# An attention and gated feed-forward layer on one core: rows of shifts sent by ScalarE's queue, every row masked on VectorE, loads and last steps in another order

## The chip, the cores and the metric

The kernel runs on one core of a Trainium2 chip. The metric is the device time of one execution in microseconds (us), as the median of several runs; lower is better. A core has TensorE (PE, matrix products), VectorE (DVE), ScalarE (ACT), GpSimd (POOL) and SyncE (SP), which run their own instruction streams and meet at semaphores, and 16 DMA engines. Products land in eight PSUM banks of 128 x 512 words.

## The reference

The input x is [4, 512, 1024]: four batches of 512 rows. One layer is computed:

```python
x = x + layernorm(attention(layernorm(x)))
x = x + layernorm(ffn(layernorm(x)))

# attention: 32 query heads and 8 key/value heads of 32, rotary q and k, causal softmax, output product
qkv = x @ w_qkv.T + b_qkv
attn = softmax(where(causal, q @ k.T / sqrt(32), -1e20)); out = (attn @ v) @ w_o.T + b_o

# ffn: base product, plus the two best of 8 experts of rank 16, weighted by a softmax of the gate
result = x @ base_w.T + base_b + 2.0 * sum_e w_full[e] * (x @ lora_A[e].T) @ lora_B[e].T
```

## The kernel before

The 2048 rows are 16 tiles of 128 (`NT`). Each f32 product is made of three products of halves: a high part (`_h`, rounded to fp32r) and the rest (`_l`). So every operand is split by a ScalarE copy (high) and a subtraction on VectorE or GpSimd (low).

There are three stages. **Projection**, to about 300 us: for each batch five pairs of q/k columns and four v tiles; rotated q and k and v go to scratch in HBM. **Attention**, to about 620 us: 32 groups (4 batches x 8 key heads), one a step; a group's q and k come back from HBM into one of four slots (`load_group`). **Output and feed-forward**, to the end: tile by tile the output product, a layer norm, the gated feed-forward (`ffn`, in three column blocks `FFN_COLS`), its low-rank part (`lora`), a layer norm and the store.

A step of attention for group n, in the order that `ORDER` writes out for TensorE:
- R0 to R10 (`row_scores`, L1345): scores of group n+2 with queries on partitions, only to find each row's maximum (`maxima` on VectorE). Later groups are masked in that operation by adding the table `row_mask` (L1015). For groups 0 and 1, whose rows are computed amid the projection of the last batch ("priming"), TensorE adds the mask with one more product of the identity and `causal_r` (L1351), and VectorE takes a plain maximum (L1020).
- T (`shift_transpose`): the maxima of group n+1 are turned into rows, split by ScalarE (`shift_to_hi`, L810) and VectorE (`shift_lo`, L1027), and written by two DMAs (`load_shift`, L494, 8 KB each, SyncE's queue) as two more rows of q in that group's slot. So the scores come out with the maximum subtracted.
- S0 to S9 (`scores`, L1371): scores of group n with keys on partitions; three banks take turns, so each S waits for the exponential (`exps`, L837, ScalarE) of the S three before it.
- V0 to V3 (`weigh`, L1387) and D (`denominators`, L1407 to L1413) for group n-1: the weighted values, and the sums of exponentials, which GpSimd has masked (L699) and partly added (`add_keys`, L711).

R units and T go round four banks, so an R waits for the maximum four units before. In steps 1 to 24 ScalarE also casts a piece of w_o (`piece_hi`, L826) and GpSimd makes its low part. SyncE's queue holds all other DMAs: per step the store of the attention values and sums, the next group (960 KB), and w_o, the bias rows and feed-forward weights in given steps. The last two steps (30 and 31) put chunks of the first output tile between the scores (`ORDER_OUT`, O0 to O7), for which `split_att` (ScalarE L844, VectorE L1097) must have split the attention values.

## Time and profile before

| | us |
|---|---|
| median of 3 runs | 1037.3 (1036.18 to 1037.53) |
| the profiled execution | 1043.99 |
| its span | 1042.3 |
| TensorE's mean granted clock | 0.988 |

Times below are from the span's start of the profiled execution. An instruction's duration includes latency that overlaps the next one, so the pace is read from start to start. The granted clock is a share of 2.4 GHz: 0.50 is the lower level, 1.2 GHz. The profile has three stretches in which it is near that: from 306 us, from 402 us and from 620 us, each of a few us.

### The profile page before, as it was taken

Reading aid. Unit: us, or ns where it says so; the run is one execution under the profiler, and the core shown is the slowest. Engines: PE = TensorE matmul, PEld = TensorE weight load, DVE = VectorE, ACT = ScalarE, POOL = GpSimd, SP = SyncE. Lnnn points to the kernel's source line nnn. Section 1 sums busy time; section 2 is a strip of 40 time slices with the busy share of each in tenths; the row PEclk is TensorE's granted clock in tenths of the full one; section 3 lists DMA queues with packets and bytes.
Section 4 is the critical chain, followed back from the end, with each engine's and each line's share of the span. In section 5 each row is a group of like instructions: output and inputs, shape, how many; then the busy total and the mean of one; then the engine's idle time right before and its main releaser. Section 6 shows DMA issues by size and latency. Waiting matters only on the chain.

```text
span 1042.3 us, 17345 instructions
## 1 busy us (share of the span) xinstructions
PE 1008.5 (97%) x6414; PEld 823.2 (79%) x6414; DVE 638.7 (61%) x1882; ACT 400.9 (38%) x682; POOL 452.3 (43%) x492
## 2 busy tenths in 40 slices
PE   6999999999989998999999989999999999999995
PEld 6888898898876665666666559999999999999995
DVE  6753533334447886788888747666666666666654
ACT  6331221200126775777777754222222222222221
POOL 1453443523337986899998851111111111111110
PEclk9999999999989998999999999999999999999998
DMA  9342431246236766656555455222222222222101
GB/s 356 138 143 102 146 132 66 91 146 178 81 135 175 205 186 161 162 138 172 141 138 138 121 176 170 79 81 83 82 87 80 84 80 74 84 82 79 53 21 40
DMA packets 78787, 127.29 MB, mean 122 GB/s; under 512 B 7792, under 2 KB 47088, under 8 KB 75632
## 3 DMA queue, kind: packets, MB, share of 16 engines
q1 hardware_dynamic: 78704, 126.19, 40.4%
q8 instruction: 51, 0.84, 0.3%
q14 instruction: 32, 0.26, 0.1%
HBM read 85.27 MB, written 40.37 MB: 121 GB/s over the span
## 4 chain that ended last, share of the span: by engine, by line
PE 92%; DVE 3%; DMA 2%; POOL 1%; ACT 1%; issue 0%; SPq 0%; POOLq 0%; DVEq 0%; ACTq 0%
PE bank L1272 21%; PE bank L1274 21%; PE bank L1273 20%; PE bank L1345 8%; PE bank L1371 7%; PE bank L1387 7%; DMA q_t<-shift_l 2%; PE bank L1281 2%; PE bank L1407 2%; PE bank L1529 1%; PE bank L1413 1%; PE bank L1410 1%; DVE bank L1015 1%; DVE ln_st L953 1%; POOL ln_rs L655 0%
## 5 line engine op out<-in xcount | busy, mean ns | idle before, releaser
L1015 DVE CUSTOM_DVE_ANT_0 bank<-bank,row_mask 128x128 f32<-128x128 f32 (+1 forms) x480 | 219.5, 523 | 61.1 <-PE bank L1345 57.1
L655 POOL TENSOR_TENSOR ln_rs<-ln_ve,minus_half 128x1 f32<-128x1 f32 x64 | 61.5, 961 | 394.6 <-DVE ln_mm L958 394.6
L837 ACT ACTIVATE prob<-bank 128x512 f32<-128x512 f32 x320 | 173.8, 598 | 44.8 <-PE bank L1371 44.7
L1272 PE MATMUL bank<-wf_h,xt_h 128*128 128x384 f32 (+1 forms) x384 | 129.7, 338 | 1.8 <-DVE z L1178 1.8
L1274 PE MATMUL bank<-wf_l,xt_h 128*128 128x384 f32 (+1 forms) x384 | 130.2, 339 | 0.0
L1273 PE MATMUL bank<-wf_h,xt_l 128*128 128x384 f32 (+1 forms) x384 | 129.6, 338 | 0.0
L1345 PE MATMUL bank<-k_t,q_t 96*128 96x384 f32 (+3 forms) x512 | 126.1, 343 | 3.0 <-DVE row_top L1015 3.0
L1272 PE MATMUL bank<-xt_h,wq_h 128*128 128x512 f32 x304 | 120.5, 397 | 0.0
L1274 PE MATMUL bank<-xt_l,wq_h 128*128 128x512 f32 x304 | 118.7, 390 | 0.0
L1273 PE MATMUL bank<-xt_h,wq_l 128*128 128x512 f32 x304 | 118.5, 390 | 0.0
L1371 PE MATMUL bank<-q_t,k_t 98*128 98x512 f32 x320 | 113.3, 418 | 5.2 <-DMA q_t<-shift_l 4.6
L1345 PEld LDWEIGHTS bank<-k_t,q_t 96*128 96x128 f32 x512 | 85.1, 195 | 24.4 <-DVE row_top L1015 15.0
L699 POOL TENSOR_SCALAR_AFFINE_SELECT prob<-prob 128x512 f32<-128x512 f32 x128 | 81.1, 645 | 50.1 <-ACT prob L837 49.9
L1272 PE MATMUL bank<-wo_h,at_h 128*128 128x512 f32 x256 | 101.3, 396 | 0.0
L1274 PE MATMUL bank<-wo_l,at_h 128*128 128x512 f32 x256 | 100.1, 391 | 0.0
L1273 PE MATMUL bank<-wo_h,at_l 128*128 128x512 f32 x256 | 100.0, 390 | 0.0
L780 ACT CAST turn_h<-turn 128x512 fp32r<-128x512 f32 x40 | 24.9, 622 | 163.5 <-POOL turn L669 151.9
L711 POOL TENSOR_TENSOR key_sum<-prob 128x512 f32<-128x512 f32 x64 | 82.0, 1288 | 8.5 <-ACT prob L837 8.5
L914 ACT ACTIVATE z<-z,ln_nm,ln_rs 128x1024 f32<-128x1024 f32 (+1 forms) x17 | 20.2, 1196 | 161.4 <-POOL ln_nm L657 161.4
L1371 PEld LDWEIGHTS bank<-q_t,k_t 98*128 98x128 f32 x320 | 59.2, 194 | 28.3 <-ACT prob L837 12.9
L711 POOL TENSOR_TENSOR key_sum<-key_sum,prob 128x512 f32<-128x512 f32 x63 | 81.5, 1313 | 0.0
L669 POOL TENSOR_TENSOR turn<-turn 128x512 f32<-128x512 f32 x20 | 25.8, 1292 | 126.5 <-DVE turn L991 126.5
(118 smaller groups left out, 1944.8 us busy)
## 6 DMA issues: line engine op xcount, KB each, us to landing
q_t<-q_scratch SPq DMA_DIRECT2D x32, 512.0 KB, 5.3
q_scratch<-turn_h SPq DMA_DIRECT2D x16, 512.0 KB, 2.7
q_scratch<-turn SPq DMA_DIRECT2D x16, 512.0 KB, 2.9
q_t<-q_scratch SPq DMA_DIRECT2D x32, 256.0 KB, 5.5
att_scratch<-att SPq DMA_DIRECT2D x32, 256.0 KB, 2.4
at_raw<-att_scratch SPq DMA_DIRECT2D x16, 512.0 KB, 3.9
x<-x SPq DMA_DIRECT2D x16, 512.0 KB, 4.2
out<-z SPq DMA_DIRECT2D x15, 512.0 KB, 2.9
```

Of the source, the lines that this page charges most:

```text
L655: nc.gpsimd.tensor_tensor(ln_rs[j][:], ln_ve[j][:], minus_half[:], ALU.pow).then_inc(count, 1)
L669: nc.gpsimd.tensor_tensor(r[:, 0, 0, :], r[:, 0, 0, :], r[:, 0, 1, :], ALU.subtract).then_inc(rope_sum, 1)
L699: nc.gpsimd.affine_select(out=block_of, in_=block_of, compare_op=ALU.is_ge, fill=0.0, base=0, pattern=[[0, REP], [1, P]], channel_multipli ...
L711: nc.gpsimd.tensor_tensor(total, first, prob[n % 2][:, b, :, :], ALU.add).then_inc(prob_summed, 1)
L837: nc.scalar.activation(prob[n % 2][:, i, :, :].rearrange("p h q -> p (h q)"), bank[3 + (NS * n + i) % 3][:], ACT.Exp, scale=INV_SQRT_HD).t ...
L1015: last = nc.vector.tensor_tensor_reduce(out=row, in0=row, in1=row_mask[:, SEQ - w:SEQ], scale=1.0, scalar=LOWEST, op0=ALU.add, op1=ALU.max ...
L1272: mm(dst, a_h, w_h, start=start, stop=False, skip_group_check=True)
L1273: mm(dst, a_l, w_h, start=False, stop=False, skip_group_check=True)
L1274: return mm(dst, a_h, w_l, start=False, stop=stop, skip_group_check=True)
L1345: last = mm(dst[:, w * at:w * at + w], q_t[s][0:KROWS, h, P * qb:P * qb + P], k_t[s][0:KROWS, 0:w], start=(at == 0), stop=masked_later(n, ...
L1371: mm(bank[3 + (NS * n + i) % 3][:].rearrange("p (h q) -> p h q", q=P), k_t[s][0:KROWS + 2, P * kc:P * kc + P], q_t[s][0:KROWS + 2, :, P * ...
L1387: last = mm(bank[6][HD * h:HD * h + HD, P * kc:SEQ].rearrange("p (b q) -> p b q", q=P), v_sb[b % 2][:, kc, HD * g:HD * g + HD], prob[n % 2 ...
```

## The change

- Causal mask: the products with `causal_r` go, all rows are masked in VectorE's maximum; `row_mask` is loaded before the first groups, in a place of its own.
- `load_shift` leaves SyncE's stream. ScalarE waits for `shift_sb` and issues the two DMAs on its own queue, behind the fourth exponential of a step.
- The score banks are turned by one and step 0 waits for the last v tiles later (at its third score).
- Loads of step 8 and 10 are put in steps 9, 11 and 13; the reciprocals of a batch's sums and their store move two and three steps.
- Step 30: S7 ahead of O0; ScalarE's `split_att(0)` behind the copy of values, the shifts and exponential 5; VectorE's behind `shift_lo`.
- After step 31: one sum less on GpSimd (D takes two more blocks directly, `FIRST[2]` and the next), VectorE waits for both of GpSimd's layer norm operations, ScalarE's and VectorE's feed-forward splits stand later.
- Feed-forward: `lora_ps` counts column blocks, `ffn` waits per block; the last tile runs blocks 0 and 1, their low-rank part, then block 2, and VectorE takes half of the statistics before block 2.

The diff, cut to its core:

```diff
-ORDER_OUT = [("S0 S1 S2 V0 V1 V2 V3 T S3 S4 S5 D S6 O0 S7 O1 S8 O2 S9 O3 "
-              "O4 O5 O6 O7").split(),
+ORDER_OUT = [("S0 S1 S2 V0 V1 V2 V3 T S3 S4 S5 D S6 S7 O0 S8 O1 S9 O2 "
+              "O3 O4 O5 O6 O7").split(),
...
             if s == SLOTS - 1:
+                row_mask = m("row_mask", [P, SEQ])
                 m = Map(e_at + SPILL, e_size - SPILL)
...
-        def masked_later(n, i):
-
-            return n >= 2
+        def score_bank(n, i):
+
+            return bank[3 + (NS * n + i + 1) % 3]
...
-            def load_shift(n):
-                s = n % SLOTS
-                sp.wait_ge(shift_sb, n + 1)
-                for i, part in enumerate((shift_h, shift_l)):
-                    dst = q_t[s][KROWS + i:KROWS + i + 1, :, :].bitcast(F32)
-                    sp.dma_start(dst, part[n % 2][:].bitcast(F32)).then_inc(shift_loaded[s], 16)
...
                     if b == BATCH - 1 and p == 0:
+                        sp.wait_ge(proj_ps, 2 * USES * (BATCH - 1))
+                        sp.dma_start(row_mask[:], row_mask_h).then_inc(mask_loaded, 16)
                         for n in range(SLOTS):
                             load_group(n)
...
-                    if b == BATCH - 1 and p == 3:
-                        load_shift(0)
...
-            sp.wait_ge(proj_ps, PROJECTED)
-            sp.dma_start(row_mask[:], row_mask_h).then_inc(mask_loaded, 16)
             load_v(0)
...
                 elif t == 1:
+                    sp.wait_ge(row_max, NR * NG)
                     sp.wait_ge(score_ps, NS * (NG - 1))
...
-                if n + 1 < NG:
-                    load_shift(n + 1)
...
-                if n >= KV and n % KV == 2:
+                if n >= KV and n % KV == 5:
                     store_inverses(n // KV - 1)
...
-                if n == WO_LOADS:
+                if n == WO_LOADS + 1:
                     sp.dma_start(bo_row[:], b_o[0].partition_broadcast(P)).then_inc(late_loaded, 16)
+                if n == WO_LOADS + 3:
                     sp.dma_start(bf_row[:], b_ffn[0].partition_broadcast(P)).then_inc(late_loaded, 16)
-                if n == WO_LOADS + 2:
+                if n == WO_LOADS + 5:
...
+            load_res(0)
             sp.wait_ge(score_ps, NS * NG)
             load_ffn(3)
             sp.dma_start(before[:], before_h[0].partition_broadcast(P)).then_inc(late_loaded, 16)
-            load_res(0)
...
-                add_keys(n, 2, total[:, 1, :, :], None, SCORES.index((2, 3)))
                 if n < NG - 1:
+                    add_keys(n, 2, total[:, 1, :, :], None, SCORES.index((2, 3)))
                     add_keys(n, 3, total[:, 0, :, :], None, FIRST[2])
...
+            def load_shift(n):
+
+                s = n % SLOTS
+                act.wait_ge(shift_sb, n + 1)
+                for i, part in enumerate((shift_h, shift_l)):
+                    dst = q_t[s][KROWS + i:KROWS + i + 1, :, :].bitcast(F32)
+                    act.dma_start(dst, part[n % 2][:].bitcast(F32)).then_inc(shift_loaded[s], 16)
...
+            load_shift(0)
...
                 exps(n, 2)
-                if n == NG - 2:
-                    split_att(0)
                 if 0 < n < NG - 1:
                     copy_values(n - 1)
                 if n + 1 < NG:
                     shift_to_hi(n + 1)
                 exps(n, 3)
+                if n + 1 < NG:
+                    load_shift(n + 1)
                 exps(n, 4)
                 if 1 <= n <= NPIECE:
                     piece_hi(n - 1)
                 exps(n, 5)
+                if n == NG - 2:
+                    split_att(0)
...
             split_ffn(3)
+            normalise_x1(0)
             copy_sums(NG - 1)
+            transposed2(0)
             split_ffn(4)
-            normalise_x1(0)
             split_ffn(5)
-            transposed2(0)
...
-            nc.vector.tensor_copy(ident_r[:], ident[:]).then_inc(const_ready, 1)
-            nc.vector.tensor_copy(causal_r[:], causal[:]).then_inc(const_ready, 1)
...
                 s = 9 * t
-                dve.wait_ge(lora_ps, t + 1)
                 wait(dve, out_stored, 16 * t)
                 for b, (at, w) in enumerate(FFN_COLS):
                     lo = max(at, AGW)
+                    if t == NT - 1 and b == 2:
+                        dve.wait_ge(z_step, s + 2)
+                        nc.vector.bn_stats(ln_st[1][:, 0, :], z[:, 0:HALF]).then_inc(z_step, 1)
+                    dve.wait_ge(lora_ps, 3 * t + b + 1)
...
+                if t == NT - 1:
+                    dve.wait_ge(z_step, s + 4)
+                    nc.vector.bn_stats(ln_st[1][:, 1, :], z[:, HALF:D]).then_inc(z_step, 1)
+                    moments(1, z_step, s + 3)
...
                 maxima_of(0, 1, 2)
+                if n + 1 < NG:
+                    shift_lo(n + 1)
                 if n == NG - 2:
                     split_att(0)
-                if n + 1 < NG:
-                    shift_lo(n + 1)
                 maxima_of(3, 4, 5)
-                if n >= KV and n % KV == 2:
+                if n >= KV and n % KV == 4:
                     invert_sums(n // KV - 1)
...
-            dve.wait_ge(y_scale, 1)
+            dve.wait_ge(y_scale, 2)
             split_att(1)
             split_ffn(2)
             residual1(0)
-            dve.wait_ge(y_scale, 3)
+            dve.wait_ge(y_scale, 4)
             split_ffn(3)
-            split_ffn(4)
             project_bias(1, 0)
             lo2(0)
+            split_ffn(4)
...
-                              start=(at == 0), stop=masked_later(n, i), skip_group_check=True)
-                if masked_later(n, i):
-                    last.then_inc(row_ps, 1)
-                    return
-                diagonal = dst[:, 0:len(heads) * w].rearrange("p (h k) -> p h k", k=w)[:, :, P * qb:w]
-                mm(diagonal, ident_r[:], causal_r[:].unsqueeze(1).broadcast_to([P, len(heads), P]), start=False,
-                   stop=True, skip_group_check=True).then_inc(row_ps, 1)
+                              start=(at == 0), stop=True, skip_group_check=True)
+                last.then_inc(row_ps, 1)
...
                     if n == 0:
                         pe.wait_ge(k_ones, SLOTS)
-                        pe.wait_ge(evac, EVACS * BATCH)
+                if n == 0 and i < 3:
+                    pe.wait_ge(evac, EVACS * BATCH if i == 2 else evacs(USES * (BATCH - 1) + PAIRS))
...
-                pe.wait_ge(prob_summed, SUMS * n + (SUMS if n < NG - 1 else 3))
+                pe.wait_ge(prob_summed, SUMS * n + (SUMS if n < NG - 1 else 2))
...
-            def ffn(t):
-                wait(pe, z_step, 9 * (t - 1) + 3)
-                for b, (at, w) in enumerate(FFN_COLS):
+            def ffn(t, blocks=range(3)):
+                for b in blocks:
+                    at, w = FFN_COLS[b]
+                    wait(pe, z_step, 9 * (t - 1) + b + 1)
...
-                ffn(t)
+                if t < NT - 1:
+                    ffn(t)
+            ffn(NT - 1, (0, 1))
             transpose_low(NT - 1)
-            lora(NT - 1)
+            lora(NT - 1, (0, 1))
+            ffn(NT - 1, (2,))
+            lora(NT - 1, (2,))
```

On ScalarE, step 1 of attention, before (numbers behind names tell buffers apart: prob_126 and prob_123 are the same buffer of the two programs):

```order
L837 ACTIVATE prob_126<-bank 128x512 x3
L854 COPY att_123<-bank 128x512
L810 ACTIVATE shift_h_76<-bank 16x128
L837 ACTIVATE prob_126<-bank 128x512 x2
L826 CAST wo_h<-wo_raw 128x384
L837 ACTIVATE prob_126<-bank 128x512
L859 COPY den_sb<-bank 128x512
L837 ACTIVATE prob_126<-bank 128x512 x4
```

and now:

```order
L831 ACTIVATE prob_123<-bank 128x512 x3
L848 COPY att_120<-bank 128x512
L795 ACTIVATE shift_h_74<-bank 16x128
L831 ACTIVATE prob_123<-bank 128x512
L804 DMA q_t_113<-shift_h_74 1x16x128
L804 DMA q_t_113<-shift_l_76 1x16x128
L831 ACTIVATE prob_123<-bank 128x512
L820 CAST wo_h<-wo_raw 128x384
L831 ACTIVATE prob_123<-bank 128x512
L853 COPY den_sb<-bank 128x512
L831 ACTIVATE prob_123<-bank 128x512 x4
```

The two DMAs, and the wait for VectorE's low part in front of them, stand between the fourth and fifth exponential; they stood on SyncE's stream. On ScalarE, step 30, before:

```order
L837 ACTIVATE prob_120<-bank 128x512 x3
L844 CAST at_h<-at_raw 128x1024
L854 COPY att_124<-bank 128x512
L810 ACTIVATE shift_h_77<-bank 16x128
L837 ACTIVATE prob_120<-bank 128x512 x3
L859 COPY den_sb<-bank 128x512
L837 ACTIVATE prob_120<-bank 128x512 x4
```

and now:

```order
L831 ACTIVATE prob_118<-bank 128x512 x3
L848 COPY att_121<-bank 128x512
L795 ACTIVATE shift_h_75<-bank 16x128
L831 ACTIVATE prob_118<-bank 128x512
L804 DMA q_t_116<-shift_h_75 1x16x128
L804 DMA q_t_116<-shift_l_77 1x16x128
L831 ACTIVATE prob_118<-bank 128x512 x2
L838 CAST at_h<-at_raw 128x1024
L853 COPY den_sb<-bank 128x512
L831 ACTIVATE prob_118<-bank 128x512 x4
```

`at_h`, from which the output product starts, has moved behind the copy of values, the shifts, the DMAs and three exponentials. On TensorE, the last tile's end, before:

```order
L1274 MATMUL bank<-wf_l_149,xt_h 128x384
L1548 MATMUL bank<-ident,low 128x128
L1272 MATMUL bank<-wo_h,low_h 128x256
L1273 MATMUL bank<-wo_h,low_l 128x256
L1274 MATMUL bank<-wo_l,low_h 128x256
L1272 MATMUL bank<-wo_h,low_h 128x384
L1273 MATMUL bank<-wo_h,low_l 128x384
L1274 MATMUL bank<-wo_l,low_h 128x384
L1272 MATMUL bank<-wo_h,low_h 128x384
L1273 MATMUL bank<-wo_h,low_l 128x384
L1274 MATMUL bank<-wo_l,low_h 128x384
```

and now:

```order
L1273 MATMUL bank<-wf_l_146,xt_h 128x384
L1545 MATMUL bank<-ident,low 128x128
L1271 MATMUL bank<-wo_h,low_h 128x256
L1272 MATMUL bank<-wo_h,low_l 128x256
L1273 MATMUL bank<-wo_l,low_h 128x256
L1271 MATMUL bank<-wo_h,low_h 128x384
L1272 MATMUL bank<-wo_h,low_l 128x384
L1273 MATMUL bank<-wo_l,low_h 128x384
L1271 MATMUL bank<-wf_h_137,xt_h 128x384
L1272 MATMUL bank<-wf_h_137,xt_l 128x384
L1273 MATMUL bank<-wf_l_145,xt_h 128x384
```

The transpose of `low` and six of the nine low-rank products now stand ahead of column block 2, whose first three products are the last rows shown; 21 more and block 2's three low-rank products follow.

## Rows read from the trace of the kernel before

**Rows 1.** Section 1 of the page: busy us (share of the span) and instructions of each engine.

```profile
PE 1008.5 (97%) x6414; PEld 823.2 (79%) x6414; DVE 638.7 (61%) x1882; ACT 400.9 (38%) x682; POOL 452.3 (43%) x492
```

**Rows 2.** Waits of TensorE over the span: line waited for, us in total, times, longest.

```profile
PE bank L1371 <- DMA q_t<-shift_l: 4.6, 4, 3.7
```

**Rows 3.** Stretch after the start of attention: us, then each engine's busy us, granted clock, DMA.

```profile
306.00:317.00 11.00, 10.62 (x36) 7.32 (x40) 8.65 (x38) 5.54 (x10) 7.36 (x8) 0.53 0.62 165
```

**Rows 4.** Chain that ended last, attention: start us, us, what ran.

```profile
324.14 0.69 PE bank L1345 x6
...
333.33 0.69 PE bank L1345 x6
...
351.70 0.69 PE bank L1345 x6
352.86 2.29 PE bank L1387 x32
...
425.00 0.69 PE bank L1345 x6
```

**Rows 5.** Timeline of one step, all engines: start, us, engine, line, operation, [idle before].

```profile
475.53 1.08 ACT L837 ACTIVATE prob<-bank 128x512 f32<-128x512 f32 x2 [0.32 <-PE bank L1371]
475.56 0.28 DVE L1027 SCALAR_TENSOR_TENSOR shift_l<-bank,shift_h 16x128 fp32r<-16x128 f32 x1
...
475.87 0.53 SPq L494 DMA_DIRECT2D q_t<-shift_h  x1
...
476.43 0.59 SPq L494 DMA_DIRECT2D q_t<-shift_l  x1
476.50 0.51 ACT L826 CAST wo_h<-wo_raw 128x384 fp32r<-128x384 f32 x1
...
477.70 0.59 ACT L859 COPY den_sb<-bank 128x512 f32<-128x512 f32 x1 [0.18 <-PE bank L1413]
...
478.18 1.16 ACT L837 ACTIVATE prob<-bank 128x512 f32<-128x512 f32 x2
...
478.78 0.62 PE L1371 MATMUL bank<-q_t,k_t 98*128 98x512 f32 x2
```

**Rows 6.** Timeline of TensorE in the projection of the last batch.

```profile
243.31 0.22 PE L1351 MATMUL bank<-causal_r,ident_r 128*128 128x128 f32 x1
243.37 0.45 PE L1272 MATMUL bank<-xt_h,wq_h 128*128 128x512 f32 x1
```

**Rows 7.** Timeline of VectorE at the start of attention.

```profile
304.90 0.30 DVE L1015 CUSTOM_DVE_ANT_0 bank<-bank,row_mask 128x128 f32<-128x128 f32 x1 [3.60 <-DMA row_mask<-row_mask]
...
307.39 0.28 DVE L1027 SCALAR_TENSOR_TENSOR shift_l<-bank,shift_h 16x128 fp32r<-16x128 f32 x1
```

**Rows 8.** Timelines at the end of attention: TensorE.

```profile
595.62 0.64 PE L1407 MATMUL bank<-prob,ones 128*32 128x256 f32 x8 [1.32 <-ACT att L854]
...
597.38 0.40 PE L1272 MATMUL bank<-wo_h,at_h 128*128 128x512 f32 x1
...
620.65 1.08 PE L1407 MATMUL bank<-prob,ones 128*32 128x256 f32 x8 [2.88 <-POOL key_sum L711]
...
623.80 0.60 PE L1272 MATMUL bank<-wo_h,at_h 128*128 128x512 f32 x1
```

**Rows 9.** Timeline at the end of attention: ScalarE.

```profile
593.94 1.05 ACT L844 CAST at_h<-at_raw 128x1024 fp32r<-128x1024 f32 x1 [1.91 <-DVE at_raw L1092]
```

**Rows 10.** Timeline at the end of attention: VectorE.

```profile
595.02 1.69 DVE L1097 TENSOR_TENSOR at_l<-at_raw,at_h 128x1024 fp32r<-128x1024 f32 x1 [1.11 <-ACT at_h L844]
```

**Rows 11.** Timeline of the last tile: TensorE.

```profile
1018.05 0.45 PE L1272 MATMUL bank<-wf_h,xt_h 128*128 128x392 f32 x1 [1.77 <-DVE z L1178]
```

**Rows 12.** Timeline of the last tile: VectorE.

```profile
1016.65 1.34 DVE L1178 TENSOR_TENSOR z<-bank,bf_row 128x256 f32<-128x256 f32 x3
...
1033.48 1.35 DVE L1178 TENSOR_TENSOR z<-bank,bf_row 128x256 f32<-128x256 f32 x3 [1.76 <-PE bank L1274]
1034.87 1.29 DVE L953 BATCH_NORM_STATS2 ln_st<-z 128x6 f32<-128x512 f32 x2
```

More of the change, by code:

```diff
@@ L122, in final_cols, with build @@
     return [slice(0, HALF), slice(HALF, D)] if t == NT - 1 else [slice(0, D)]
-def build(nc, x, w_qkv, b_qk, b_v, w_out, b_o, w_ffn, b_ffn, cos_t, sin_t, ident_h, causal_h, row_mask_h, before_h, out):
+def build(nc, x, w_qkv, b_qk, b_v, w_out, b_o, w_ffn, b_ffn, cos_t, sin_t, ident_h, row_mask_h, before_h, out):
     q_scratch = nc.dram_tensor("q_scratch", [BATCH, PAIRS - 1, 2, 2, P, SEQ], F32).ap()
@@ L953, in statistics, with moments @@
                     nc.vector.bn_stats(ln_st[j][:, h, :], src[:, HALF * h:HALF * h + HALF]).then_inc(count, 1)
+                moments(j, count, before_it)
+            def moments(j, count, before_it):
                 dve.wait_ge(count, before_it + 2)
@@ L1006, in maxima @@
                 w = P * (qb + 1)
+                if n == 0 and i == 0:
+                    dve.wait_ge(mask_loaded, 16)
                 dve.wait_ge(row_ps, NR * n + i + 1)
@@ L1009, in maxima @@
                     wait(dve, shift_ps, n - 1)
-                if masked_later(n, i):
-                    if n == 2:
-                        dve.wait_ge(mask_loaded, 16)
-                    for at, h in enumerate(heads):
-                        row = row_bank(n, i)[:, w * at:w * at + w]
-                        last = nc.vector.tensor_tensor_reduce(
-                            out=row, in0=row, in1=row_mask[:, SEQ - w:SEQ], scale=1.0, scalar=LOWEST,
-                            op0=ALU.add, op1=ALU.max, accum_out=row_top[n % 2][:, h, qb:qb + 1])
-                    last.then_inc(row_max, 1)
-                else:
-                    nc.vector.tensor_reduce(row_top[n % 2][:, heads[0]:heads[-1] + 1, qb],
-                                            row_bank(n, i)[:, 0:len(heads) * w].rearrange("p (h k) -> p h k", k=w), AX_X, ALU.max
-                                            ).then_inc(row_max, 1)
+                for at, h in enumerate(heads):
+                    row = row_bank(n, i)[:, w * at:w * at + w]
+                    last = nc.vector.tensor_tensor_reduce(
+                        out=row, in0=row, in1=row_mask[:, SEQ - w:SEQ], scale=1.0, scalar=LOWEST,
+                        op0=ALU.add, op1=ALU.max, accum_out=row_top[n % 2][:, h, qb:qb + 1])
+                last.then_inc(row_max, 1)
             def shift_lo(n):
@@ L1179, in ffn_sum @@
                                             ).then_inc(z_step, 1)
-                dve.wait_ge(z_step, s + 3)
-                statistics(z, 1, z_step, s + 3)
+                if t == NT - 1:
+                    dve.wait_ge(z_step, s + 4)
+                    nc.vector.bn_stats(ln_st[1][:, 1, :], z[:, HALF:D]).then_inc(z_step, 1)
+                    moments(1, z_step, s + 3)
+                else:
+                    dve.wait_ge(z_step, s + 3)
+                    statistics(z, 1, z_step, s + 3)
             def residual2(t):
@@ L1403, in denominators @@
                     pe.wait_ge(den_ready, n)
+                if n == 0:
+                    pe.wait_ge(const_ready, 1)
                 p, total = prob[n % 2], key_sum[n % 2]
@@ L1417, in denominators @@
                         dst = den_bank(n)[HD * h:HD * h + HD, :].rearrange("p (b q) -> p b q", q=P)
-                        last = mm(dst[:, 2:3, :], ones[:], p[:, FIRST[2]:FIRST[2] + 1, h, :], start=False, stop=True,
+                        last = mm(dst[:, 2:4, :], ones[:], p[:, FIRST[2]:FIRST[2] + 2, h, :], start=False, stop=True,
                                   skip_group_check=True)
@@ L1548, in transpose_low, with lora @@
                 nc.tensor.transpose(bank[7][:, 0:P], low[:].rearrange("p e r -> p (e r)"), ident[:]).then_inc(low_ps, 1)
-            def lora(t):
+            def lora(t, blocks=range(3)):
                 pe.wait_ge(low_ready, t + 1)
-                for b, (at, w) in enumerate(FFN_COLS):
+                for b in blocks:
+                    at, w = FFN_COLS[b]
                     lo = max(at, AGW)
@@ L1556, in lora @@
                                    False, True)
-                last.then_inc(lora_ps, 1)
+                    last.then_inc(lora_ps, 1)
             project_out(1, 0)
```

15 lines of the change are left out of this document (2 added, 13 removed).

## The prediction

> **What bounds the kernel now.** I read the page's busy shares first: TensorE is busy for 97% of the span [rows 1], so nothing counts unless it takes work from TensorE, fills one of its waits, or makes a new one. The list of TensorE's waits is next: behind the unavoidable start, the rows of shifts are its largest cause, 4.6 us in four waits [rows 2]. But a wait costs more than its length where the clock falls after it: from 306 to 317 us the granted clock is 0.53, near its lower level of 1.2 GHz, and what came before is TensorE's wait for the first maximum, which itself waited for the mask table [rows 3, 7]. So I measure stalls by the period of a step on the chain of waits. An undisturbed step takes 333.33 - 324.14 = 9.19 us. From 351.70 to 425.00 there are seven steps: 73.3 us where 64.3 are due, so the late shifts cost 9.0 us, clock included [rows 4]. In the timeline of a step I then look for what ScalarE has to spare, since the change gives it work.
>
> **The change part by part.** The sum is made against the profiled execution's 1043.99 us and taken off the median of 1037.3 us unchanged; the profile ran 6.7 us longer than the median, so some stalls in it may be the profile's own.
>
> Causal products (22 of them, 11 units for two groups). The next product starts 0.06 us after one of 128 columns, and that next one takes 0.45 us instead of the 0.40 of its kind, a weight load laid bare [rows 6]. 0.12 x 22 = 2.6 us, and 3.0 with the six that are 256 and 512 columns wide. Bounds: 0, if the place were a wait in disguise, and 22 x 0.22 = 4.8 by the whole duration. I take -3.0, as TensorE has no wait there. VectorE gets 32 masked maxima for 22 plain ones; the projection keeps TensorE the bound and VectorE waits for it there.
>
> Start of attention. The mask table is now loaded with the first groups, before the priming. VectorE's first maxima start where its wait of 3.60 us began, at 301.3, not at 304.90, and with them `shift_lo`: 307.39 - 3.6 = 303.8 [rows 7]. ScalarE then issues the DMAs for 1.15 us, to 305.0 (durations below), and has six exponentials of step 0 left at 0.51 each, start to start: 308.1. Step 1's weighted values wait for its S1 and S2, behind these: 308.8. Such a block starts 352.86 - 351.70 = 1.16 us after its step's first R, so step 2's first R stands at 308.8 - 1.16 + 9.19 = 316.8, and 317.4 with step 1's own share of the delay below, for 324.14 [rows 4]: -6.7. Bounds: 0 and -8.
>
> Shift stalls. Before, the two 8 KB DMAs stood in line behind a group's 960 KB and, around step 8, three more loads of 512 KB. Those are now in steps of their own, and the rows have their own queue. I take -8.0 of the 9.0; bounds 0 (all of it the profile's own, or carried over) and -9.0.
> The Trainium skill says on this, in "DMA: Bandwidth & Descriptors", section "Issuing engines are not separate DMA queues", that DMAs of all engines run on the same 16 DMA engines and interleave, and that using several saves the issuing time only. No row here shows two queues at once. By this rule the queue would cure nothing and the spreading of the loads alone most of it, so the sum would lose the small stalls (a rival below).
>
> ScalarE's new work. On SyncE the two issues last 0.53 and 0.59 us and follow each other: 475.87 to 477.02 [rows 5]. No row shows an issue on ScalarE; bounds are 0 and that 1.15. I take the latter. The DMAs wait for `shift_lo`, ended at 475.84. Exponential 4, the second of the pair at 475.53, began at 476.02 and would now at 477.05: 1.03 late. Behind it the cast, exponential 5, the copy of the sums and exponential 6 queue. ScalarE had 0.18 us idle before that copy, so 0.85 is left at exponential 6, which ended at 478.18 + 0.60 = 478.78. S9, the second of the pair at 478.78, starts at 479.01 and needs it, 0.23 later. So TensorE stops for 0.62 us in each such step. It is not carried on: behind the weighted values ScalarE sits idle, and starts the next step level. Of the steps with a cast, 2 to 24 count here: 23 x 0.62 = 14.3. The five without (25 to 29) have the cast's 0.51 to spare: 5 x 0.1 = 0.5. Together +14.8; bounds 0 and 28 x 1.03 = 28.8.
> "Perfetto Trace Analysis" of the Trainium skill, section on the HWDGE DMA instruction, has the profiled window of an issue end when the sequencer is free for the next instruction. The trace agrees on SyncE, where the next issue starts 0.03 us behind the first. By the rule ScalarE loses the whole 1.15 us, as in the sum; were it free of this, the sum would be that of the second rival.
>
> Step 30. D no longer waits for ScalarE's copy, which was held by `at_h` (1.32 us goes) [rows 8]. But `at_h` moves from 593.94 [rows 9] behind the shifts (594.2 to 594.5), their DMAs (595.65) and exponentials 4 and 5: 596.7. `at_l` starts at its end, took 1.69 us and, beside less of GpSimd's work, may take somewhat less [rows 10]: 599.2. O0 stood at 597.38 and, with S7 (0.23 us) now in front of it, would stand at 599.2: a net +1.6. TensorE waits there from 596.6, 2.6 us. A wait of that length has lowered the clock twice [rows 3, 8]; the last of these made D take 3.15 us (620.65 to 623.80) for some 1.6 at full clock, so +1.5. Bounds +0.5 and +4.
>
> After step 31. D waited 2.88 us for GpSimd's last sum and ran at the lower clock; it would start at 617.8 and end at 619.5, for 623.80 [rows 8]: -4.3. What is late next is `at_l` of tile 1, held by `ln_nm` now: 618.5, in time. Bounds -1 and -5.
>
> Last tile. `ffn` waits for one of three additions (0.45 of 1.34 us): -0.9 of the 1.77 [rows 11, 12]. At the end two of three additions and one of two statistics (0.9 + 0.65) are hidden by block 2's 24 products: -1.5 [rows 12]. Together -2.4, bounds -1 and -3.
>
> The rest (reciprocals, loads' places, constants) I cost at nothing: VectorE and SyncE are not the bound there. If that cover fails, it costs a fraction of a us four times.
>
> Sum: -3.0 - 6.7 - 8.0 + 14.8 + 3.1 - 4.3 - 2.4 = -6.5. 1043.99 becomes 1037.5, and 1037.3 becomes 1030.8 us.
>
> **The rivals.**
> The issue is cheap on ScalarE. For it: no row shows it there. Against: two issues on SyncE never overlap. The +14.8 goes, and the total is -21.3: 1016.0 us.
>
> ScalarE becomes the bound. Should the idle time before the copy and S9's 0.23 not absorb anything, or an issue take longer where SyncE issues too, the delay per step grows. The gains are 21.3 us over 28 steps: from 0.76 us a step on the kernel is slower. With the whole 1.03, it is 28.8 - 21.3 = +7.5: 1044.8 us. For it: ScalarE's instructions from exponential 4 to 6 stand without a gap but one. Against: the 0.18 and 0.23 us are measured.
>
> The rows land no sooner. Large loads on the same engines delay them as before; the stalls around step 8 may go by the spread loads, the others stay, and where they were the profile's own nothing goes: between -8.0 and 0. With 0 the total is +1.5: 1038.8 us. Against: the small stalls too stand where the queue is full.
>
> The start does not gain: step 0 has thin work on TensorE, the clock may fall there anyway. It took 11 us at 0.53; I price it at +2.5: 1033.3 us.
>
> **How the numbers follow.** Chances: forecast, with the thin start in it, 0.55; cheap issue 0.17; ScalarE the bound 0.16; rows no sooner 0.12. A measurement of this kernel can tell about 0.2%, 2 us. The forecast's own range is 1025 to 1037; 0.47 of its 0.55 lies more than 2 us under 1037.3, 0.06 within, 0.02 above. Cheap issue is all faster. The bound case is slower, 0.14, or the same, 0.02. Rows no sooner: 0.04 faster, 0.06 the same, 0.02 slower. Faster 0.68, same 0.14, slower 0.18. The range for 8 in 10 runs from 1017 to 1042: it leaves out the cheapest issue and the worst delay.
>
> **What would show it.** ScalarE's DMA issues would have durations near 0.5 us, exponential 4 would start about 1 us behind the issue, and TensorE would show 23 waits near 0.6 us for ScalarE's exponential, a period near 9.8 us up to step 24, and 9.2 to 9.3 from 25 on. No wait for the shift rows, and none for the mask. No L1351. A wait of about 2.6 us before the first product of the output with a low clock behind it; none before D of group 31. The last addition would follow the last product by 0.2 us and half of the statistics would be gone from the tail. I am wrong if the period stays 9.19 (cheap issue), or reaches 10.2.

## The result, and the profile after

The changed kernel takes **1047.93 us** in the median of 6 runs (1046.74 to 1050.94). The kernel before, run beside it, takes 1037.41 us (1035.17 to 1040.05). The ratio is 1.0104, with a 95% interval of 1.0084 to 1.0124: slower by 1%, where 1030.8 us and a gain were forecast, and above the range of 1017 to 1042. The profiled execution took 1048.65 us (span 1046.9), 4.7 more than the one before. That one ran 6.6 us above its own median, so the traces show less of the loss than the times do.

Section 1 of the page after, first line; then two lines of the list of TensorE's waits, in the columns of [rows 2]:

```profile
PE 1009.8 (96%) x6392; PEld 815.0 (78%) x6392; DVE 645.2 (62%) x1922; ACT 398.5 (38%) x682; POOL 446.6 (43%) x491
```

```profile
PE bank L1365 <- ACT prob L831: 11.2, 27, 0.5
...
PE bank L1365 <- DMA q_t<-shift_l: 1.7, 3, 1.1
```

TensorE has 22 products fewer than in [rows 1], and as much busy time. The wait for the shift rows of [rows 2] has shrunk from 4.6 to 1.7 us. A new wait stands on top: 27 times, 0.41 us on average, for ScalarE's exponential.

The chain of waits after, read as [rows 4]: step 2, and then three neighbouring steps with a cast.

```profile
317.10 0.68 PE bank L1343 x6
...
376.73 0.69 PE bank L1343 x6
...
386.61 0.68 PE bank L1343 x6
...
396.47 0.69 PE bank L1343 x6
```

Step 2 starts at 317.10, where 324.14 stood before. That this is next to the forecast's 317.4 is luck: the 317.4 held the gain of the start alone, and with the 3.0 us of the causal products it should have been 314.4. But above all a step now lasts 386.61 - 376.73 = 9.88 us instead of 9.19. The timeline of such a step shows why; the columns are those of [rows 5]:

```profile
483.99 0.60 ACT L831 ACTIVATE prob<-bank 128x512 f32<-128x512 f32 x1 [0.32 <-PE bank L1365]
484.02 0.28 DVE L1022 SCALAR_TENSOR_TENSOR shift_l<-bank,shift_h 16x128 fp32r<-16x128 f32 x1
...
484.33 0.51 ACTq L804 DMA_DIRECT2D q_t<-shift_h  x1
...
484.87 0.61 ACTq L804 DMA_DIRECT2D q_t<-shift_l  x1
...
485.52 0.60 ACT L831 ACTIVATE prob<-bank 128x512 f32<-128x512 f32 x1 [0.94 <-issue]
...
486.02 0.50 ACT L820 CAST wo_h<-wo_raw 128x384 fp32r<-128x384 f32 x1
...
486.42 0.60 ACT L831 ACTIVATE prob<-bank 128x512 f32<-128x512 f32 x1
...
486.91 0.58 ACT L853 COPY den_sb<-bank 128x512 f32<-128x512 f32 x1
...
487.38 2.08 ACT L831 ACTIVATE prob<-bank 128x512 f32<-128x512 f32 x4
...
487.23 0.40 PE L1365 MATMUL bank<-q_t,k_t 98*128 98x512 f32 x1
488.05 0.50 PE L1365 MATMUL bank<-q_t,k_t 98*128 98x512 f32 x1 [0.41 <-ACT prob L831]
```

This is the mechanism that was forecast. ScalarE issues for 0.51 and 0.61 us. Exponential 4 starts 0.04 us behind the second issue and 0.94 us later than it could have. The cast, exponential 5 and the copy pass the delay on, and the score product S9 waits for exponential 6, which began at 487.38. The wait of 0.41 us costs more than its length: S9 starts 0.82 us behind S8 (487.23) where it was 0.23 before (478.78 and 479.01), and lasts 0.50 us instead of 0.40. Together that is the 0.69 us.

At the start of attention the wait for the mask table goes, as was expected. First the window of [rows 3], then VectorE's maxima and `shift_lo`, as in [rows 7], then TensorE in front of step 1:

```profile
306.00:317.00 11.00, 9.87 (x85) 6.12 (x86) 7.56 (x34) 6.80 (x15) 7.77 (x9) 1.00 0.47 117
```

```profile
299.08 0.30 DVE L1014 CUSTOM_DVE_ANT_0 bank<-bank,row_mask 128x128 f32<-128x128 f32 x1 [0.21 <-PE bank L1343]
...
301.57 0.27 DVE L1022 SCALAR_TENSOR_TENSOR shift_l<-bank,shift_h 16x128 fp32r<-16x128 f32 x1
```

```profile
306.72 0.50 PE L1365 MATMUL bank<-q_t,k_t 98*128 98x512 f32 x1 [1.06 <-DMA q_t<-shift_l]
```

The wait for the table is gone, and the granted clock stays at its upper level, 1.00 where it was 0.53. What the prediction lacked is the last line: it let step 1 start as soon as ScalarE's exponentials were done and expected no wait for the shift rows, but the low row, issued at 302.42, landed 4.3 us later, and TensorE waited for it.

The end of attention after: TensorE, which answers to [rows 8]; ScalarE and VectorE, [rows 9, 10]; and one window with the granted clock.

```profile
601.55 0.64 PE L1403 MATMUL bank<-prob,ones 128*32 128x256 f32 x8 [1.11 <-POOL key_sum L696]
...
605.57 0.71 PE L1271 MATMUL bank<-wo_h,at_h 128*128 128x512 f32 x1 [1.85 <-DVE at_l L1088]
...
627.27 0.64 PE L1403 MATMUL bank<-prob,ones 128*32 128x256 f32 x8
...
629.13 0.50 PE L1271 MATMUL bank<-wo_h,at_h 128*128 128x512 f32 x1
```

```profile
602.87 1.05 ACT L838 CAST at_h<-at_raw 128x1024 fp32r<-128x1024 f32 x1
```

```profile
603.95 1.57 DVE L1088 TENSOR_TENSOR at_l<-at_raw,at_h 128x1024 fp32r<-128x1024 f32 x1 [3.28 <-ACT at_h L838]
```

```profile
603.00:610.00 7.00, 5.15 (x18) 3.78 (x15) 3.93 (x2) 3.58 (x6) 4.87 (x5) 0.76 0.26 78
```

O0 waits 1.85 us for `at_l`, and D had to wait 1.11 us for GpSimd before it; a lower clock follows, as forecast. D of group 31 waits for nothing and is done in 1.86 us, for 3.15 in [rows 8].

The last tile after, TensorE and VectorE, for [rows 11, 12]:

```profile
1023.89 0.45 PE L1271 MATMUL bank<-wf_h,xt_h 128*128 128x392 f32 x1 [0.86 <-DVE z L1172]
```

```profile
1034.30 1.02 DVE L1172 TENSOR_TENSOR z<-bank,bf_row 128x256 f32<-128x256 f32 x2 [0.78 <-PE bank L1273]
1035.35 0.69 DVE L1169 BATCH_NORM_STATS2 ln_st<-z 128x6 f32<-128x512 f32 x1
...
1039.48 0.56 DVE L1172 TENSOR_TENSOR z<-bank,bf_row 128x384 f32<-128x384 f32 x1 [3.44 <-PE bank L1273]
```

Two additions and one of the statistics now lie beside products, and `ffn` waits 0.86 instead of 1.77 us.

### The profile page after: what moved, and what is told of

It is laid out like the page before. It is cut to its first block, busy times and chain, and to the rows that moved or that the text cites. A ratio compares the mean times of both kernels' runs of the same rounds, so it can differ in the third digit from the quotient of the medians.

```text
span 1046.9 us, 17330 instructions
## 1 busy us (share of the span) xinstructions
PE 1009.8 (96%) x6392; PEld 815.0 (78%) x6392; DVE 645.2 (62%) x1922; ACT 398.5 (38%) x682; POOL 446.6 (43%) x491
## 4 chain that ended last, share of the span: by engine, by line
PE 83%; ACT 7%; DVE 3%; ACTq 2%; DMA 2%; issue 2%; POOL 1%; POOLq 0%; DVEq 0%
PE bank L1271 20%; PE bank L1273 20%; PE bank L1272 20%; PE bank L1381 7%; PE bank L1343 6%; PE bank L1365 5%; ACT prob L831 4%; ACTq L804 2%; DMA q_t<-shift_l 2%; PE bank L1280 1%; PE bank L1525 1%; ACT wo_h L820 1%; ACT den_sb L853 1%; POOL ln_rs L640 1%; DVE ln_st L949 1%
## 5 line engine op out<-in xcount | busy, mean ns | idle before, releaser
L1014 DVE CUSTOM_DVE_ANT_0 bank<-bank,row_mask 128x384 f32<-128x384 f32 (+3 forms) x512 | 236.0, 519 | 90.2 <-PE bank L1343 89.6
L831 ACT ACTIVATE prob<-bank 128x512 f32<-128x512 f32 x320 | 175.3, 610 | 68.7 <-PE bank L1365 38.6
L1365 PE MATMUL bank<-q_t,k_t 98*128 98x512 f32 x320 | 119.7, 423 | 13.1 <-ACT prob L831 11.2
L1343 PE MATMUL bank<-k_t,q_t 96*128 96x384 f32 (+3 forms) x512 | 123.5, 337 | 0.4 <-DVE row_top L1014 0.3
L1343 PEld LDWEIGHTS bank<-k_t,q_t 96*128 96x128 f32 x512 | 82.8, 190 | 21.6 <-DVE row_top L1014 7.9
L696 POOL TENSOR_TENSOR key_sum<-key_sum,prob 128x512 f32<-128x512 f32 x62 | 77.9, 1276 | 0.0
```

Source lines behind the costliest of these rows:

```text
L696: nc.gpsimd.tensor_tensor(total, first, prob[n % 2][:, b, :, :], ALU.add).then_inc(prob_summed, 1)
L831: nc.scalar.activation(prob[n % 2][:, i, :, :].rearrange("p h q -> p (h q)"), score_bank(n, i)[:], ACT.Exp, scale=INV_SQRT_HD).then_inc(pr ...
L1014: last = nc.vector.tensor_tensor_reduce(out=row, in0=row, in1=row_mask[:, SEQ - w:SEQ], scale=1.0, scalar=LOWEST, op0=ALU.add, op1=ALU.max ...
L1343: last = mm(dst[:, w * at:w * at + w], q_t[s][0:KROWS, h, P * qb:P * qb + P], k_t[s][0:KROWS, 0:w], start=(at == 0), stop=True, skip_group ...
L1365: mm(score_bank(n, i)[:].rearrange("p (h q) -> p h q", q=P), k_t[s][0:KROWS + 2, P * kc:P * kc + P], q_t[s][0:KROWS + 2, :, P * qb:P * qb ...
```

## The experiments

"Period" is the time from one step's first R to the next one's. "Excess" is the sum of the periods from step 2 on, less 9.19 us each (step 28 is the last with such a period): 8.9 us in the first profile of before and 21.6 us in that of after. What is left behind the last such mark is the "end part": 461.3 and 460.2 us.

**The shift rows back on SyncE (e1_syncq, and again e11_syncq_again).**

```diff
-                act.dma_start(dst, part[n % 2][:].bitcast(F32)).then_inc(shift_loaded[s], 16)
+                sp.dma_start(dst, part[n % 2][:].bitcast(F32)).then_inc(shift_loaded[s], 16)
```

with `load_shift(n + 1)` first in SyncE's step n, as before; all else stays as changed.

> The changed kernel with one thing undone: both rows of shifts are issued by SyncE again, at the start of a step; all else as changed. Theory A (each step's two issues keep ScalarE for 1.04 us, of which 0.69 us in steps with a cast and 0.27 us in those without reach TensorE, 17 us in all): the step is 9.19 us again, no wait of TensorE for ScalarE's exponentials, and the time falls by 17 us less the stalls that ScalarE's queue had removed (0 to 5): 1031 to 1036 us, under the kernel before. Rival B (the loss comes from the other edits: the turned banks, the spread loads, the masks, the last steps): the time stays within 3 us of 1048.

> The changed kernel with the rows of shifts issued by SyncE once more, beside the two others. 1022 to 1024 us, ratio 0.983 to 0.985. If step 30 in its new order costs something (the run with the old order had 0.9834), this ratio is over 0.9845; if it gains, under 0.983.

1022.91 us, ratio 0.9837 (0.9817 to 0.9857); measured again, 1022.36, ratio 0.9841 (0.9825 to 0.9857). So this one part of the change, the issuing engine, costs 25 us by the medians, 27 by the ratios, and without it the change is a gain of 1.6%. Both theories missed the size: theory A, which is right on the steps, had 1031 at the least. No kernel tried here is faster by more than can be told. The periods are 9.19 us again, the excess is 1.8 and 1.05 us, step 0 takes 7.16 us instead of 8.58, and the end part is 457.3 to 457.7. ScalarE's exponentials, from the fifth section of the pages, of after and of e1_syncq:

```profile
L831 ACT ACTIVATE prob<-bank 128x512 f32<-128x512 f32 x320 | 175.3, 610 | 68.7 <-PE bank L1365 38.6
```

```profile
L833 ACT ACTIVATE prob<-bank 128x512 f32<-128x512 f32 x320 | 173.3, 599 | 35.9 <-PE bank L1365 35.9
```

The idle time before them is 68.7 us with the issues on ScalarE and 35.9 without. Of the 68.7, the trace puts 30.0 down to "issue", the rest to TensorE.

**ScalarE's queue alone (e2_scalarq_alone):** the kernel before, with `load_shift` on ScalarE and nothing else.

> The kernel before with one thing done: the two rows of shifts are issued by ScalarE behind exponential 3; all else as before. Theory A: a step of 9.88 us with the cast and 9.47 without, +17 us, less the stalls of the kernel before that the queue removes (about 2 in an undisturbed run, up to 9): 1046 to 1053 us. Rival B: within 3 us of the kernel before, 1035 to 1040.

1062.49 us, ratio 1.0211 (1.0189 to 1.0232): 22 us more than before, above what either theory gave. The waits of TensorE, two lines:

```profile
PE bank L1371 <- ACT prob L835: 10.5, 25, 0.5
...
PE bank L1371 <- DMA q_t<-shift_l: 2.5, 1, 2.5
```

The periods are 9.88 with a cast, and two of 12.85 and 12.74 us stand at steps 9 and 10, with the granted clock low behind the wait. The excess is 24.7 us: 17.0 from the delay of each step, as in the changed kernel, and 7.7 from long steps. The end part is 464.9 us, some 4 us longer than in the two profiles of before: D of step 30 waits 2.1 us for GpSimd's sum, where it waited 1.3 for ScalarE's copy. Theory A had left out the end part and taken the queue to remove long steps. The rows had the queue to themselves and still landed late there. By the Trainium skill, "DMA: Bandwidth & Descriptors", section "Issuing engines are not separate DMA queues", DMAs issued by different engines run on the same 16 DMA engines and interleave. The trace agrees, with this wait of 2.5 us in spite of the rows' own queue.

**One row each (e3_half):** the changed kernel, `shift_h` issued by SyncE and `shift_l` by ScalarE.

```diff
-                for i, part in enumerate((shift_h, shift_l)):
+                for i, part in ((1, shift_l),):
```

> The changed kernel with one of the two rows (the high part) issued by SyncE and the other still by ScalarE. Theory A: ScalarE loses 0.5 to 0.6 us a step instead of 1.04, of which 0.18 idle before its copy and some 0.2 before the tenth score take most: at most 0.2 us reaches TensorE in a step with a cast, nothing without, so the step is 9.2 to 9.4 us and the time 1031 to 1038. A rival in which any issue on ScalarE stops it for a fixed time whatever it sends (a drain of its pipeline) expects the period of 9.88 to fall by half of 0.69 or less: 9.5 us or more, 1040 or more.

1024.28 us, ratio 0.9849 (0.9831 to 0.9867), period 9.25 with a cast and 9.19 without. The period is as theory A had it; its time, 1031 us or more, was too high, as in e1_syncq. One issue, of 0.52 us here, costs 0.06 us a step, two cost 0.69: ScalarE has spare time for nearly all of one, and only what exceeds it reaches TensorE. The rival of a fixed stop at any issue falls.

**The cast out of the way (e10_cast_late):** the changed kernel with both issues on ScalarE, and

```diff
                 exps(n, 4)
-                if 1 <= n <= NPIECE:
-                    piece_hi(n - 1)
...
                 for i in range(6, NS):
                     exps(n, i)
+                if 1 <= n <= NPIECE:
+                    piece_hi(n - 1)
```

> The changed kernel as it is, both rows of shifts issued by ScalarE, with one edit: the cast of a piece of w_out (0.50 us) stands behind the last exponential of the step, where ScalarE is idle, and no longer behind exponential 4. Theory A (the two issues delay exponential 6 by what they last less ScalarE's spare time before S9, so spare time given back is time gained): the periods of steps 2 to 24 fall from 9.88 to 9.47, as in the steps without a cast; 23 x 0.41 = 9.4 us, and some of the stalls with it: 1034 to 1039 us, ratio 0.995 to 1.000. Theory B (the issues cost by something else, as traffic or the clock): the periods stay at 9.8 to 9.9 and the time at 1045 to 1050.

1037.14 us in the median of 12 runs, ratio 0.999 (0.9978 to 1.0003): 10.8 us less than the changed kernel. The periods are 9.47 to 9.6 in most steps, and TensorE's list has a wait for an exponential twice instead of 27 times. The 0.28 us by which these steps still exceed 9.19 shows in the periods alone. Its waits, one line:

```profile
PE bank L1365 <- ACT prob L831: 0.9, 2, 0.5
```

Nothing about the DMAs differs, so theory B falls: it is ScalarE's time between exponentials 3 and 6 that counts.

**Spreading the loads alone (e5_spread_alone):** the kernel before, with `bo_row`, `bf_row`, `load_ffn(6)` and the inverses' store in later steps.

> The kernel before with one part of the change: bo_row, bf_row, load_ffn(6) and the inverses' store (with invert_sums) in later steps of their own; the rows of shifts stay on SyncE with everything else. The stalls of steps 8 to 12 took 8.9 us in the first profile of before and 3.2 us in its second. Theory A (they come from the rows standing in line behind these loads): the stalls go, the periods of all steps from 2 on are within 0.5 us of 9.19, and the time is 2 to 6 us below the kernel before, ratio 0.994 to 0.998. Theory B (rows are late for another reason, the 960 KB group and the chance order in the engines): stalls of 10 us and more remain near steps 9 to 11, ratio 0.999 to 1.001.

1033.74 us, ratio 0.9951 (0.9936 to 0.9966), 5 us faster. The wait for the shift rows in its trace:

```profile
PE bank L1372 <- DMA q_t<-shift_l: 0.2, 1, 0.2
```

The excess is 0.5 us, with the rows in SyncE's queue among all others. The stalls came from the loads that stood beside them, as theory A has it.

**The kernel before, profiled again (before_again).** One execution of 1035.58 us (span 1033.9) and the same wait:

```profile
PE bank L1371 <- DMA q_t<-shift_l: 2.2, 1, 2.2
```

The excess is 3.2 us, for 8.9 in the first profile. So 6 of the 9.0 us that the prediction wanted back were missing in this execution. It is quicker, though, than all nine executions of this kernel that were timed beside it (1037.95 to 1042.59), as the first profile is longer than any of them. The 5 us of e5_spread_alone, from medians, are the better measure of the stalls.

D of group 31 waits in it as in [rows 8], but does not run slowly, and the window around it has the upper clock:

```profile
612.90 0.64 PE L1407 MATMUL bank<-prob,ones 128*32 128x256 f32 x8 [2.88 <-POOL key_sum L711]
```

```profile
611.00:616.00 5.00, 3.10 (x38) 2.36 (x39) 1.96 (x3) 2.25 (x3) 1.80 (x1) 1.00 0.87 331
```

The next five undo one more part each (the last of them two) in the kernel with the rows on SyncE, which has 1022.36 us and ratio 0.9841 as its reference.

**Step 30 as before (e6_old_step30).**

```diff
-ORDER_OUT = [("S0 S1 S2 V0 V1 V2 V3 T S3 S4 S5 D S6 S7 O0 S8 O1 S9 O2 "
+ORDER_OUT = [("S0 S1 S2 V0 V1 V2 V3 T S3 S4 S5 D S6 O0 S7 O1 S8 O2 S9 O3 "
```

and both `split_att(0)` where they were.

> The changed kernel with the rows of shifts issued by SyncE, and step 30 as before: O0 in front of S7, ScalarE's split_att(0) behind exponential 2, VectorE's in front of shift_lo. Compared with the same kernel with the new step 30 (1022.9 us, ratio 0.9837). Theory A (the prediction's +3.1 for the new step 30, less about 0.6 since ScalarE no longer issues there): the old order is better, 1020 us, ratio 0.981, and the new one showed its clock drop in 603 to 610 as the cost. Theory B: what O0 waits for at_l is paid back by D no longer waiting for at_h, and the two orders are equal: 1022 to 1024, ratio 0.983 to 0.985. Theory C: the new order is better by 1 to 3 us: 1024 to 1026.

1022.01 us, ratio 0.9834 (0.9819 to 0.9848): no difference to be told. With SyncE issuing, O0 waits 1.3 us for `at_l` in the new order, and D waits 1.3 us for ScalarE's copy, held by `at_h`, in the old one. Theory B holds: the two waits are exchanged. D waits another 0.8 us for GpSimd in the new order; the end part is 456.4 us in the old order and 457.3 to 457.7 in the new, too little to show in the times.

**The work behind step 31 as before (e7_old_after31).**

```diff
-                if n < NG - 1:
-                    add_keys(n, 2, total[:, 1, :, :], None, SCORES.index((2, 3)))
+                add_keys(n, 2, total[:, 1, :, :], None, SCORES.index((2, 3)))
...
-                pe.wait_ge(prob_summed, SUMS * n + (SUMS if n < NG - 1 else 2))
+                pe.wait_ge(prob_summed, SUMS * n + (SUMS if n < NG - 1 else 3))
```

with the waits and splits of `w_ffn` behind it.

> The changed kernel with the rows of shifts issued by SyncE, and the work behind step 31 as before: GpSimd adds the third sum for group 31 and D waits for three sums, VectorE waits for y_scale 1 and 3, and the splits of w_ffn stand as before on ScalarE and VectorE. Theory A (the prediction's -4.3 for this part of the change): 1027 us, ratio 0.988, with a wait of 2 to 3 us before D and a lower clock behind it. Theory B (the profile of after gave back only 1.1 us in all from step 30 on, the waits move to ScalarE's normalised y): 1023 to 1025, ratio 0.984 to 0.986.

1025.07 us, ratio 0.9868 (0.9852 to 0.9884), between the two theories: the part is worth 2.7 us. D of group 31 in its timeline, and the window around it:

```profile
604.11 0.64 PE L1403 MATMUL bank<-prob,ones 128*32 128x256 f32 x8 [2.88 <-POOL key_sum L708]
...
605.76 0.50 PE L1271 MATMUL bank<-wo_h,at_h 128*128 128x512 f32 x1
```

```profile
603.41:608.41 5.00, 4.30 (x44) 3.33 (x45) 4.23 (x7) 1.56 (x2) 1.94 (x3) 1.00 0.84 300
```

The wait is exactly that of [rows 8], but the clock stays at 1.00 and D takes 1.65 us, not 3.15, just as in before_again, where the kernel is the same as in [rows 8]. The same window in the first trace of before:

```profile
620.00:625.00 5.00, 4.34 (x37) 2.61 (x38) 2.93 (x6) 1.71 (x3) 1.04 (x2) 0.66 0.69 270
```

The low clock behind such a wait is not a fixed part of its price.

**The last tile as before (e8_old_last_tile).**

```diff
-            ffn(NT - 1, (0, 1))
-            transpose_low(NT - 1)
-            lora(NT - 1, (0, 1))
-            ffn(NT - 1, (2,))
-            lora(NT - 1, (2,))
+            transpose_low(NT - 1)
+            lora(NT - 1)
```

with `ffn` in one piece, waiting for all three additions, and additions and statistics in one piece too.

> The changed kernel with the rows of shifts issued by SyncE, and the feed-forward's ends as before: ffn waits for all three additions of the tile before it, the last tile's three blocks go in one piece, its additions and statistics wait for the last of them. Theory A (the prediction's -2.4 for this part): 1025.3 us, ratio 0.986, the time behind the last product 1.5 us longer and the wait before ffn 0.9 longer. Theory B: only the end counts, 1.5 us, or the reordered last tile's products pay it back: 1023 to 1024.

1026.66 us, ratio 0.9882 (0.9869 to 0.9895): the part is worth 4.3 us, more than theory A's 2.4. The first product behind the wait, and the window behind it:

```profile
998.70 0.44 PE L1263 MATMUL bank<-wf_h,xt_h 128*128 128x392 f32 x1 [1.79 <-DVE z L1169]
```

```profile
999.50:1004.50 5.00, 5.00 (x21) 5.00 (x21) 2.11 (x5) 1.24 (x1) 0.74 (x2) 0.66 0.00 0
```

This time the clock did fall behind the wait, to 0.66 for 5 us, 1.7 us of work. In the trace of before the same wait left it at 1.00. The end part of this trace, 461.3 us, is 4.0 longer than in e1_syncq: 0.9 by the wait, 1.4 behind the last product, and these 1.7. So in this trace the clock accounts for what the part is worth beyond waits and tail. All four timed runs have the same mean granted clock, 0.996, as the profiled one, where the reference has 0.997 to 0.999, so it probably fell in all of them; but only one has a trace.

**The causal products back (e9_causal_products_back).**

```diff
+                diagonal = dst[:, 0:len(heads) * w].rearrange("p (h k) -> p h k", k=w)[:, :, P * qb:w]
+                mm(diagonal, ident_r[:], causal_r[:].unsqueeze(1).broadcast_to([P, len(heads), P]), start=False,
+                   stop=True, skip_group_check=True).then_inc(row_ps, 1)
```

for groups 0 and 1, with their plain maxima.

> The changed kernel with the rows of shifts issued by SyncE, and with the causal products of groups 0 and 1 and their plain maxima back; the mask table still comes early. Compared with the same kernel without them, run beside it. Theory A (the prediction's -3.0, 0.12 us and more for each of 22 products on TensorE while nothing waits): 3 us slower, 1026 us, ratio 0.9865, and the first R of step 0 stands at 301.5 to 302.5 instead of 298.4. Theory B (VectorE's 10 additional masked maxima had cost what the products save, the gain of the start is all from the early mask): less than 1 us apart. Step 0 takes 7.2 to 7.5 us in both by either theory, since the mask is no longer waited for.

1025.0 us, ratio 0.9868 (0.9853 to 0.9883): the products cost 2.6 us, as in theory A.

**The mask table late as well (e12_mask_late):** e9, with the load of `row_mask` behind the projection as before.

> As the kernel with the causal products of groups 0 and 1 back (1025.0 us, ratio 0.9868; rows of shifts on SyncE), and with the mask table's load where it stood before: behind the last product of the projection. Compared with that kernel, this is what the earlier mask alone is worth. Theory A (the prediction's -6.7 for the start): 1031 to 1032 us, ratio 0.993, with the wait of 3 us for the first maxima and the granted clock near 0.5 for some 10 us behind it. Theory B (the sum of the other parts as timed leaves only 2 to 3 us for it, since the first profile had the longest clock drop): 1027 to 1028.5, ratio 0.989 to 0.990; steps 0 and 1 together 18.9 to 20.5 us against 16.6.

1029.93 us, ratio 0.9914 (0.9898 to 0.993), 4.9 us above e9 and between the two theories. VectorE's first maximum there, and the window of [rows 3]:

```profile
305.07 0.30 DVE L1024 CUSTOM_DVE_ANT_0 bank<-bank,row_mask 128x128 f32<-128x128 f32 x1 [3.47 <-DMA row_mask<-row_mask]
```

```profile
306.00:317.00 11.00, 10.44 (x65) 7.29 (x65) 9.46 (x45) 6.43 (x13) 7.39 (x8) 0.84 0.65 187
```

The wait for the table is nearly that of [rows 7] (3.60), yet the clock fell to 0.84 here and to 0.53 there. The early mask takes the wait away in either case; how far the clock falls behind that wait varies.

## Why the prediction was wrong

**The step that failed: ScalarE's issue, +14.8 forecast, +25 measured** (25.0 and 25.6 by the two runs on SyncE). The mechanism was right and the size was not. The +14.8 stood for the steps from 2 on; there the trace of after and that of e1_syncq differ by 21.6 - 1.8 = 19.8 us.

Of these, 17.0 are the direct part, which was nearly right. The delayed steps lose 0.69 us (0.62 forecast) and the others 0.28 (0.1): 23 x 0.69 + 4 x 0.28 = 17.0. Both the late exponential 6 and the cast's share in it are shown, by e3_half and e10_cast_late.

The other 2.8 us are single long steps, which the prediction put at nothing with "It is not carried on". The traces show two causes. In steps 10, 13, 20 and 26 the second issue itself lasted 0.82, 1.33, 0.73 and 0.93 us instead of 0.61. In the last three of them the step is longer by just that excess: 0.72, 0.12 and 0.32 us (step 10 by 0.9 us, with waits of its own). Three steps of e2_scalarq_alone and one of e10_cast_late show the same, each to 0.01 us. On SyncE such an issue costs nothing: e1_syncq has one of 1.32 us in step 13, and that step lasts 9.19 us. And step 11 is 1.6 us longer, with a granted clock of 0.66 from 407 to 412 us, behind two waits of TensorE in step 10 (0.48 us for an exponential, 0.42 for the shift rows); e1_syncq has 1.00 all through attention.

The rest of the 25 us lies outside those steps: 1.4 us in step 0, 0.7 in step 1, and 3.0 in the end part. The latter is mostly the wait for `at_l` (1.9 for 1.3 us), D's for GpSimd (1.1 for 0.8) and the clock of 0.76 for 7 us (1.7 us), where e1_syncq has 1.00. The prediction had some of this, in its terms for the start and for step 30, so 14.8 should be set against 19.8, and not against the whole 25.

I had bounded the term at 28.8, so the size was in the bounds. But I gave the rival by which ScalarE becomes the bound 0.16 and a time of 1044.8; with the 25 us in place of 14.8, the sum of the prediction is +3.7, past break-even.

**Shift stalls, -8.0 forecast.** The spreading of the loads alone brought 5 us, and the queue none that its one trace shows: in e2_scalarq_alone the long steps stay. The prediction named both ways, the profile's own stalls and the rule on queues, and took the optimistic end. It sized the term on one long execution: the same kernel had 8.9 us of excess in one profile and 3.2 in the other.

**Causal products, -3.0:** 2.6 measured, right.

**Start of attention, -6.7:** the wait for the table went and the clock stayed at 1.00, as said, but the early mask is worth 4.9 us. Start and causal products together were to bring step 2 forward by 9.7 us; the traces have 324.14 - 317.10 = 7.0. Step 1 waited for the shift rows, a wait that the forecast's path had left out. The trace that it was sized on had the deepest fall of the clock of the five that have this wait: 0.53, where the others have 0.69 (e5_spread_alone) to 0.84 (e12_mask_late).

**Step 30, +3.1:** seen in the trace of after, O0's wait with a low clock behind it. With the rows on SyncE the wait is 1.3 us for 1.9, the clock stays at 1.00, and the new order costs nothing that can be told. The fall of the clock there came with the issues.

**After step 31, -4.3:** 2.7. The wait of 2.9 us went, as said. The 1.5 for the clock is not bound to it: e7_old_after31 and before_again have the same wait and D at full clock. And the next waits came up: 1.1 us for the normalised y and 0.5 for `low` in e1_syncq, which e7 has not or has at 0.2.

**Last tile, -2.4:** 4.3. The 0.9 of the wait and 1.4 of the tail are in the traces; the rest is likely the clock (1.7 in the trace of e8_old_last_tile), which was left out here and counted in for step 31.

The parts as timed are 5.1 + 2.6 + 4.9 + 2.7 + 4.3 = 19.6 us of gain, and all of them together gave 16 to 17; each has an interval of some 1.5 us. Against the 21.3 of the prediction that is 4 to 5 short, and the issue cost 10 more. Both errors are on the same side, the larger is the issue, and the 2 us still missing to the measured +10.5 lie within these intervals.

## What to carry to other kernels

Giving an engine DMAs to issue is giving it work: look for the engine's spare time between the issue and the next result that the bounding engine needs, and count what exceeds it in every step (one issue of 0.5 us cost 0.06 us a step here, two cost 0.69, and 25 us of 1048 in all). Size a gain on stalls and low clocks only from two profiles of the same kernel, since one execution here had 6 us of stalls that the next had not. And here the late rows were cured by taking away the loads that travelled beside them, not by another queue.

## What the runs showed of the hardware

An issue of one 8 KB row on ScalarE lasts 0.51 us for the first and 0.61 for the second (medians of 32), at most 1.33, and the next activation starts 0.04 us behind it. It holds up ScalarE's computing for its whole length, the long ones too: 1.33 us instead of 0.61 made the step 0.72 us longer.

The granted clock behind a wait of TensorE is not fixed by the wait. Behind the same wait of 2.9 us it stayed at 1.00 in e7_old_after31 and in before_again, and was 0.66 over 620 to 625 in the first trace of before, whose kernel is that of before_again. Behind 1.8 us in the last tile it was 1.00 in before and 0.66 in e8_old_last_tile.
